# GpSimd's subtractions wait for VectorE's weighing of the same step, except in the steps that weigh a tile's first chunk

## What is computed

```python
def _gat_layer(x, W, adj):          # x 4096x256, W 256x512, adj 4096x4096
    proj = x @ W
    Wh, Ws = jnp.split(proj, 2, axis=-1)
    scores = Wh @ Ws.T
    a = jax.nn.softmax(scores, axis=-1) * adj
    out = a @ Wh
    out = out + x
    return jax.nn.leaky_relu(out, 0.01)

y = x
for l in range(2):
    y = _gat_layer(y, W_stack[l], adj)
return _layernorm(x + y, axis=-1)
```

## Time and profile before

| | us |
|---|---|
| median of 3 runs | 1756.03 |
| lowest and highest | 1752.26, 1757.13 |
| the profiled execution's own time | 1754.34 |
| its span in the trace | 1752.4 |

### The profile page before, as it was taken

The page is one execution under the profiler, slowest core; times in us unless marked ns, Lnnn a source line. Parts: engine busy times, 40 slices in busy tenths (PEclk is TensorE's granted clock), DMA queues, the critical chain, the costliest instruction groups (busy, mean ns, idle before and its releaser), DMA issues.

```text
span 1752.4 us, 23469 instructions
## 1 busy us (share of the span) xinstructions
PE 1609.2 (92%) x8104; PEld 1322.0 (75%) x8104; DVE 1267.1 (72%) x1558; ACT 677.0 (39%) x1175; POOL 935.8 (53%) x935
## 2 busy tenths in 40 slices
PE   7799999999999999997789999999999999998996
PEld 6787888887888888886677777777777777777774
DVE  4668777777777777766357777778777778777775
ACT  4344344344443433443233433333333433333332
POOL 2456555555555565554445555555555555555554
PEclk9999999999999999999899999999999999999998
DMA  5367777777777777788325766776766776776774
GB/s 174 95 165 187 182 182 197 185 178 182 182 194 183 198 185 180 182 215 217 94 84 144 186 167 171 185 191 163 183 163 175 185 187 163 181 184 158 184 189 109
DMA packets 167750, 302.59 MB, mean 173 GB/s; under 512 B 39760, under 2 KB 68432, under 8 KB 167504
## 3 DMA queue, kind: packets, MB, share of 16 engines
q1 hardware_dynamic: 106192, 133.28, 31.7%
q0 software_dynamic: 36864, 134.23, 26.8%
q10 hardware_dynamic: 24576, 33.59, 8.3%
HBM read 157.29 MB, written 9.44 MB: 95 GB/s over the span
## 4 chain that ended last, share of the span: by engine, by line
PE 45%; DVE 35%; POOL 5%; ACTq 5%; ACT 5%; issue 4%; DMA 1%; SPq 0%; POOLq 0%
PE banks L395 15%; DVE ring L614 10%; DVE neg_max L586 8%; PE banks L294 7%; PE banks L397 7%; PE banks L296 7%; PE banks L295 7%; DVE ring L619 6%; POOL a_lo L700 5%; ACTq L194 5%; ACT a_hi L507 2%; DVE rows L627 1%; DVE rows L629 1%; DVE rows L631 1%; DVE q_t L550 1%
## 5 line engine op out<-in xcount | busy, mean ns | idle before, releaser
L700 POOL TENSOR_TENSOR a_lo<-turned,a_hi 128x512 fp32r<-128x512 f32 x512 | 737.7, 1455 | 637.2 <-ACT a_hi L507 637.0
L395 PE MATMUL banks<-wh,a_hi 128*128 128x512 f32 x2048 | 764.9, 411 | 108.6 <-POOL a_lo L700 103.4
L488 ACT ACTIVATE ring<-banks,neg_max 128x1024 f32<-128x1024 f32 x256 | 286.1, 1117 | 866.1 <-DVE neg_max L586 866.1
L395 PEld LDWEIGHTS banks<-wh,a_hi 128*128 128x128 f32 x2048 | 389.7, 190 | 262.7 <-POOL a_lo L700 157.4
L397 PE MATMUL banks<-wh,a_lo 128*128 128x256 f32 x2048 | 579.7, 283 | 0.0
L586 DVE TENSOR_REDUCE neg_max<-banks 128x1 f32<-128x1024 f32 x256 | 309.8, 1210 | 273.9 <-PE banks L296 273.8
L614 DVE SCALAR_TENSOR_TENSOR ring<-ring,weight,load 128x1024 f32<-128x1024 f32 x256 | 412.9, 1613 | 12.3 <-DMA load<-adj 9.6
L294 PE MATMUL banks<-x_t,q_t 128*128 128x512 f32 x1024 | 405.0, 396 | 5.6 <-DVE x_t L550 4.0
L296 PE MATMUL banks<-x_t,q_t 128*128 128x512 f32 x1024 | 401.4, 392 | 0.0
L295 PE MATMUL banks<-x_t,q_t 128*128 128x512 f32 x1024 | 401.3, 392 | 0.0
L397 PEld LDWEIGHTS banks<-wh,a_lo 128*128 128x128 f32 x2048 | 392.1, 191 | 4.6
(11 more groups left out here) (66 smaller groups left out, 727.4 us busy)
## 6 DMA issues: line engine op xcount, KB each, us to landing
load<-adj POOLq DMA_DIRECT2D x256, 512.0 KB, 5.2
turned<-ring SPq DMA_DIRECT2D x1536, 64.0 KB, 4.1
turned<-ring ACTq DMA_DIRECT2D x512, 64.0 KB, 4.0
ring<-x SPq DMA_DIRECT2D x8, 512.0 KB, 5.4
rows<-x SPq DMA_DIRECT2D x32, 128.0 KB, 3.4
x_scratch<-rows SPq DMA_DIRECT2D x32, 128.0 KB, 3.6
ring<-x_scratch SPq DMA_DIRECT2D x8, 512.0 KB, 5.2
rows<-x_scratch SPq DMA_DIRECT2D x32, 128.0 KB, 4.4
```

What stands on the lines that cost most here:

```text
L395: nc.tensor.matmul(psum[:, bank, :], a_hi[:, s, b], wh[:, k].rearrange("p a d -> p (a d)"), start=start, stop=stop, skip_group_check=True)
L488: nc.scalar.activation(ring[:, i % RING, :].rearrange("p (b e) -> p b e", b=2), psum[:, 2 * (i % 2):2 * (i % 2) + 2, :], ACT.Exp, bias=neg ...
L700: nc.gpsimd.tensor_tensor(a_lo[:, j % 2].rearrange("p b (r j) -> p b r j", r=QUADS), as_f32(turned[:, unit % 2, :, b:b + SUB, :]).rearrang ...
```

## The change

Before each subtraction GpSimd now also waits until VectorE has finished weighing the chunk of the same step. Chunk `j // 2` is the one being subtracted, and `weighed` is the chunk three further on, which is weighed in the same step. The wait is left out where `weighed` lies in the other layer or is the first chunk of a tile. No instruction is moved, added or taken away on TensorE, VectorE, ScalarE or SyncE, and GpSimd's work keeps its order.

```diff
             def split_a(j):
                 unit, b = j // SUB, j % SUB * SUB
                 pool.wait_ge(hi_done, j + 1)
+
+                weighed = j // 2 + LAG_PRODUCT - LAG_WEIGH
+                if weighed // CHUNKS == j // 2 // CHUNKS and weighed % CPT:
+                    pool.wait_ge(a_done, weighed + 1)
                 nc.gpsimd.tensor_tensor(
```

## The result

| | before | changed |
|---|---|---|
| median, us | 1754.91 (4 runs) | 1741.00 (4 runs) |
| lowest and highest | 1752.26, 1757.13 | 1739.24, 1742.73 |
| span of the profiled execution | 1752.4 | 1740.4 |

The ratio is 0.9926, with a 95% interval of 0.9915 to 0.9938: 13 us faster, between 11 and 15. Forecast were 1740 us and a gain of 15.1.

A forecast was written before the change was run, and what follows sets the result against it. TensorE was taken as nearly full (92% busy), with VectorE's chain ending the side steps. Terms: -15.9 (layer 1) - 4.6 (layer 0) + 3.4 (between layers) + 2.0 (semaphore) = -15.1 us, giving 1740 us, range 1733 to 1751.

The forecast's parts named there:

- The side steps: Steps with q-side work, 15 per layer: weighing before both subtractions, taking 1.28 us instead of 2.33 or 2.34, ending 1.06 earlier.
- the hole of step 180: TensorE's idle 1.52 us before step 180's first half, after side step 179: it closes and absorbs TensorE's 0.6 us lateness.
- Eight steps of layer 1: Sign to look for in the changed trace: eight steps of layer 1 take 51.3 us instead of 52.3.
- The term for layer 1: Layer 1's side steps: VectorE's chain moves up 1.06 us in each of 15, a gain of 15.9 us.
- The wake-up: GpSimd's start after the weighing ends in a side step: 0.1 us, with 0.3 still covered for TensorE.
- The semaphore: One more semaphore instruction before GpSimd's subtractions with two waits: 0.04 us in some 50 waits, 2.0 us lost.
- the prediction's lower bound: Extra semaphore before GpSimd's subtraction: costs nothing if done while `hi_done` is awaited; the upper bound was 7.5 us.
- Between the layers: Steps 129 and 130: the product starts later behind the new wait, a loss of 3.4 us, between 1.5 and 3.4.
- Layer 0: Layer 0's side steps: the maximum moves up 0.33 us in 13 of them, two with 0.5; gain 4.6 us.
- it goes down the same chain into step 40: Layer 0, behind side step 39: the 0.33 us gain reaches step 40, where TensorE idles 0.76 us for `a_lo`.
- The slower rival: Side steps: TensorE's lateness counts and VectorE's gain does not; 14.4 us slower, 1769 us; chance 7%.
- the rival that VectorE's gain is only partly handed on: Layer 1's side steps: each gives 0.46 us instead of 1.06, 6.9 in all, result 1750 us; chance 15%.

The follow-up runs named there:

- e11: The changed kernel as it is, measured a second time on one chip beside the same kernel without the wait between the layers: 0.9931 to the kernel before.
- e1: Changed kernel with the new wait only in layer 1's side steps: 0.9902 to the kernel before, 1738.47 us.
- e3: Changed kernel with the new wait only in ordinary steps, not in side steps, between the layers or at first chunks: 0.9990 to the kernel before.
- e12: Changed kernel without the new wait in steps 129 to 131, measured beside the unedited changed kernel: 0.9903 to the kernel before.
- e6: Changed kernel with the new wait only in steps 129 to 131, between the layers: 1.0017 to the kernel before, 3.0 us slower.
- e7: Changed kernel with the new wait only in layer 0's side steps: 0.9983 to the kernel before, 3.0 us faster.
- e8: Kernel before, with VectorE's weighing made to wait for both subtractions in layer 1's side steps, no new GpSimd wait: 1.0204, 36 us slower.
- e4: Changed kernel with the wait only in layer 1's side steps, there for the transpose behind the weighing too: 0.9981 to the kernel before, 3.3 us faster.
- e10: Kernel before, no new wait, with TensorE making a q side before the product from step 140 on: 0.9858, 1729.95 us.
- e2: Changed kernel without the new wait in steps 129 to 131, between the layers: 0.9890 to the kernel before, 1735.13 us.

## Why the prediction was right, and where it was not

**Where the gain is.** Right. The side steps behave as forecast to about 0.1 us: weighing 1.27, the product 1.4 later, the scores 0.7 later, the hole of step 180 closed, step 181 1.03 earlier. Eight steps of layer 1, forecast to take 51.3 us instead of 52.3, take 51.7 over the same nine periods (weighing of step 179 to that of 251) in the first profile and 51.2 in e11's. The term for layer 1 was 15.9 us; e1 alone measures 17 (15 to 19). In the first profile layer 1 gave 12.4, because 1.0 came in only nine of the fourteen eight-step periods. In steps 185 and 189 ScalarE's `a_hi` was late behind its issue of transfers, which took 1.89 and 2.42 us instead of 1.16. The kernel before has the same at its step 189 (2.13), so I do not lay it to the change.

**The wake-up.** Taken as 0.1 from `inv_std`; it is 0.15 to 0.16 for a subtraction in 14 of layer 1's 15 side steps (in step 179 by the rounded rows 0.17: the weighing ends at 1181.18, the subtraction starts at 1181.35), and 0.45 in one. It is covered.

**The semaphore.** The term was mis-sized: 2.0 us forecast, nothing measured (e3). In the 153 steps of e3 the first subtraction starts 0.09 us behind the `a_hi` it waited for, by the median, and 0.09 in the same steps of the kernel before. The step that failed is the transfer of ScalarE's row to GpSimd. In the trace the wait for `a_done` is an instruction of its own, 0.02 us long; in step 183 of the changed kernel GpSimd has it behind it at 1203.83, before the `a_hi` it needs next ends at 1204.45. This is the prediction's lower bound, "if it is done while `hi_done` is awaited". ScalarE's five waits came, as two such instructions, behind its issue of transfers, when they were all that was left to do, and there they cost 0.15. The estimate from the Trainium skill ("Advanced Engine Details and Errata", Network/Comms) of 50 to 100 ns, 2.5 to 5 us, is not borne out either.

**Between the layers.** Sign and place right, the size perhaps too small: 3.4 forecast, with 3.4 as its upper bound; 4.9 by e11 against e12, 3.0 by e6 alone, 4.5 in the first profile by step 131, and the first two take in 3.4 with their uncertainty. Against the kernel before, the product of step 129 lost 1.0 us and that of step 130 lost 2.1, together 3.1 of the 3.4. The rest came on top: from the first to the second half the two lost another 0.3 and 0.5 us, and 0.5 more up to step 131. Here TensorE ran slower behind the longer holes. The product's first matmul took 0.50 us in step 129 before, and takes 0.79 and 0.80 in steps 129 and 130 now:

```profile
822.45 0.79 PE L395 MATMUL banks<-wh,a_hi 128*128 128x512 f32 x1 [4.97 <-POOL a_lo L704]
...
834.61 0.80 PE L395 MATMUL banks<-wh,a_hi 128*128 128x512 f32 x1 [5.23 <-POOL a_lo L704]
```

All three traces with the wait have 0.79 or 0.80 at both steps. Without it, the hole of 3.5 us before step 129 is followed by 0.50 in four of eleven traces, the kernel before among them, and by 0.79 or 0.80 in seven; the 3.3 to 3.4 us before step 130 by 0.50 in nine of eleven. So the slower start in step 130 goes with the longer hole, and that in step 129 is in part the luck of the comparison. The prediction counted a hole as long as it is and put what TensorE does behind a long one at nothing.

**Layer 0.** The 0.33 us at the maximum is right (278.98 against 279.45 of the earlier trace rows, at a start that is 0.17 earlier). That it all arrives in step 41 is not. In the profile only 1.65 us of 4.6 arrive by step 127; e7 has 3.0 (0.5 to 5.4), and the kept traces together about 2.3. The step that failed is "it goes down the same chain into step 40". In step 40 the subtraction and the weighing start within 0.1 us of each other. Before, the weighing was first, and TensorE stood idle once, 0.76 before the first half. Now the subtraction is first (282.44 against 282.51), the weighing takes 2.29, and TensorE is held up at the second half and again in step 41:

```profile
282.51 2.29 DVE L614 SCALAR_TENSOR_TENSOR ring<-ring,weight,load 128x1024 f32<-128x1024 f32 x1
...
282.44 1.28 POOL L704 TENSOR_TENSOR a_lo<-turned,a_hi 128x512 fp32r<-128x512 f32 x1 [2.21 <-ACT a_hi L507]
...
290.72 0.50 PE L395 MATMUL banks<-wh,a_hi 128*128 128x512 f32 x1 [0.25 <-POOL a_lo L704]
```

Over 39 to 47 this leaves 0.06 of the 0.33 (the difference goes from -0.14 to -0.20). The order turns this way behind eight of layer 0's side steps in this profile, and what is left of the 0.33 there varies. Where it stays, as over 79 to 87 (in step 80 the weighing is first and takes 1.28 before and 1.29 after), all of it arrives (-1.13 to -1.50). In step 48 it turns the other way, from subtraction to weighing first, and 0.32 arrives (-0.20 to -0.52).

**The sum.** Layer 0 was overrated by 1.6 to 3 us and the loss between the layers perhaps underrated by 1.5, which makes the forecast too good; the semaphore was overrated by 2.0 and layer 1, by e1, perhaps underrated by 1, which makes it too bad. That 15.1 stands so near to 13.0 owes something to their cancelling. That 1740 stands even nearer to 1741.0 is luck: 0.9 us were rounded off the forecast, and the kernel before's median came out 1.1 us lower with its fourth run than with the three that the forecast started from. The slower rival, that TensorE's lateness counts and VectorE's gain does not, is refuted by e8, and e4 shows how near its point is: one more VectorE instruction of 1.3 us in front of the subtraction takes 14 of the 17 us, over half of it by the clock. Against the rival that VectorE's gain is only partly handed on stands e1: 17 us (15 to 19) over 15 side steps is all of the 1.06.

## What to carry to other kernels

When two engines take turns at something, the total hardly changes and only the order can be chosen (in step 179 the three instructions took 3.50 us from first start to last end before, and 3.93 with the order forced): give the first turn to the one whose chain ends the step, and look one step ahead for idle time that takes the other's lateness. Ask this for each kind of step apart. Here the same wait gains 1.0 us in one kind, up to 0.4 in another, nothing in most, and costs in two more. Then ask why the two meet at all: moving the q side ahead of the product on TensorE (e10) was worth more than any order of the two.

## What the runs showed of the hardware

- VectorE woken by GpSimd's subtraction started 0.10 us after its end in 15 of 16 cases and 0.45 in one (e8, the steps with the wait). GpSimd woken by VectorE's weighing started 0.15 to 0.16 us after its end in 14 of layer 1's 15 side steps and 0.45 in one (changed kernel). One step can mislead here: e8's step 179 is the odd one.
- After TensorE stood still for up to 1.65 us in layer 1's side steps (changed kernel, e1, e2, e11), its granted clock was 1.00 over the next 4 us in every one; the stretch below is the changed kernel's, from the start of step 179's product. After 2.64 us it was 1.00 in six cases and 0.57 to 0.69 in eight (e4), after 3.0 to 4.2 us 0.50 to 0.69 in all fifteen (e8). The same program and the same hole can so come with either clock, and a hole with the slower one costs more than its length: about 1.0 us more in e4.

```profile
1182.70:1186.70 4.00, 3.96 (x21) 3.44 (x22) 3.68 (x13) 2.62 (x5) 1.89 (x3) 1.00 0.54 120
```
